# Reordering the rounds of a fused attention and routing pipeline: the division of the outputs, the turns of x and of the normed rows, and two stores

## The reference

```
xn = layernorm(x)
cq, ckv = xn @ Wc + bc, xn @ Wckv + bckv                 # 128 wide each
q = [cq @ Wcq | rope(cq @ Wqr)]                          # 16 heads x 48
k = [ckv @ Wck | rope(xn @ Wkr)];  v = ckv @ Wv          # v: 16 heads x 32
scores[i, j] = q_i . k_j / sqrt(48)                      # 16 x 16 for each token
x = x + layernorm((softmax(scores) @ v) @ Wo + bo)
xf = layernorm(x)
w = softmax(xf @ gate_w.T);  top 6 of 64 experts per token, capacity 128 each
y = sum of the chosen experts' FFN(xf) * w  +  shared FFN(xf)
out = x + layernorm(y)
```

## Time and profile before

| | |
|---|---|
| median of 3 runs | 2039.34 us (2036.21 to 2047.08) |
| profiled execution | 2034.23 us, span of the instructions 2032.2 us |
| PE, PE weight loads | busy 1816.6 us (89%), 1423.7 us (70%) |
| DVE, ACT, POOL | busy 1490.3 us (73%), 1038.9 us (51%), 557.1 us (27%) |
| mean granted clock of PE | 0.974 of full speed |

### The profile page before, as it was taken

One profiled execution on the slowest core, in us unless ns is written; L12 is line 12 of the kernel. 1 busy time (PEld: TensorE's weight loads), 2 busy tenths in 40 slices (PEclk: granted clock), 3 DMA queues, 4 the chain that ended last, 5 costly groups with the idle time before them and its releaser, 6 DMA issues. The chain is left out here.

```text
span 2032.2 us, 50014 instructions
## 1 busy us (share of the span) xinstructions
PE 1816.6 (89%) x14529; PEld 1423.7 (70%) x14529; DVE 1490.3 (73%) x3935; ACT 1038.9 (51%) x2257; POOL 557.1 (27%) x773
## 2 busy tenths in 40 slices
PE   5799999999999999999999999974899999988886
PEld 4678888888888887888888888864455555546664
DVE  6678888888888888888888888863444444429997
ACT  4555656666665656666665656651222323223333
POOL 1111212111121212111121212110344444427776
PEclk8899999999999999999999999997899999989998
DMA  5345555555555555555555555546999999979994
GB/s 188 72 122 147 132 148 133 149 128 130 144 131 150 130 147 132 145 133 134 145 127 149 128 149 132 136 133 192 338 294 288 298 288 309 292 197 395 404 394 174
DMA packets 540056, 384.01 MB, mean 189 GB/s; under 512 B 423848, under 2 KB 432168, under 8 KB 539944
## 3 DMA queue, kind: packets, MB, share of 16 engines
q1 hardware_dynamic: 519456, 324.99, 55.7%
q0 software_dynamic: 14336, 35.66, 7.5%
q10 hardware_dynamic: 6208, 22.68, 2.9%
HBM read 232.46 MB, written 150.63 MB: 189 GB/s over the span
## 5 line engine op out<-in xcount | busy, mean ns | idle before, releaser
L615 ACT COPY kT<-bank 48x256 f32<-48x256 f32 x512 | 308.7, 603 | 11.0
L890 POOL TENSOR_SCALAR ve<-mv 128x1 f32<-128x1 f32 x192 | 42.2, 220 | 893.6 <-DVE mv L725 893.6
L457 PE MATMUL bank<-wgu,xfT 128*128 128x416 f32 x512 | 193.2, 377 | 18.6 <-ACT xfT L615 18.2
L615 ACT COPY qT<-bank 48x256 f32<-48x256 f32 x512 | 187.8, 367 | 33.9 <-PE bank L450 23.0
L1097 PE MATMUL e_gu<-w,xgT 128*128 128x384 f32 x512 | 183.5, 502 | 15.4 <-DMA w<-w_ed 12.4
L458 PE MATMUL bank<-wgu,xfT 128*128 128x416 f32 x512 | 183.1, 358 | 0.0
L908 POOL TENSOR_TENSOR x<-yn,xres 128x512 f32<-128x512 f32 x64 | 81.6, 1275 | 238.5 <-DVE yn L729 238.5
L1097 PEld LDWEIGHTS e_gu<-w,xgT 128*128 128x128 f32 x512 | 92.9, 191 | 74.1 <-DMA w<-w_ed 9.9
L1258 DVE SCALAR_TENSOR_TENSOR tanh<-tanh,e_gu 128x192 f32<-128x192 f32 x64 | 22.7, 354 | 165.8 <-ACT tanh L1184 165.8
L1341 POOL DMA_INDIRECT acc_scratch<-eo,sidx x64 | 101.5, 1586 | 121.4 <-ACT eo L1180 105.9
L1120 PE MATMUL e_ps<-w,hidT 96*128 96x512 f32 x256 | 127.7, 621 | 1.6 <-ACT hidT L1172 0.9
(11 more groups left out here) (178 smaller groups left out, 4849.9 us busy)
## 6 DMA issues: line engine op xcount, KB each, us to landing
w<-w_eg SPq DMA_DIRECT2D x60, 768.0 KB
acc_scratch<-zero SPq DMA_DIRECT2D x130, 256.0 KB, 4.2
w<-w_ed SPq DMA_DIRECT2D x60, 384.0 KB
xf_scratch<-xf SPq DMA_DIRECT2D x64, 288.0 KB, 2.1
xin<-x SPq DMA_DIRECT2D x64, 256.0 KB, 3.0
v_scratch<-v SPq DMA_DIRECT2D x64, 256.0 KB, 3.7
vbd<-v_scratch SPq DMA_DIRECT2D x128, 128.0 KB, 3.3
o_scratch<-o SPq DMA_DIRECT2D x256, 64.0 KB, 2.3
```

Source lines behind the costliest of these rows:

```text
L457: nc.tensor.matmul(dst, a[:, 0], b[:, 0], start=(n == 0), stop=False)
L615: nc.scalar.copy(dst, src).then_inc(done.sem, 1)
```

## The change

The operations stay the same; their order changes, with the waits in front of them.

- PE: the turn of the normed rows moves from behind the latents to the head of the round. The turn of `xn` moves from ahead of the turn of `prob` to behind the `wck` product, ahead of PV. The rank product moves ahead of PV.
- ACT: the copy of `xfT` moves to the head of the round, the exp of the gates from ahead of the `probT` copies to behind the copy of `xT`.
- DVE: the low part of `xfT` moves up behind the first statistics. `chosen`, `ssum` and `srec` move ahead of `y`. The division follows `k` directly. The low part of `xT` falls behind the division, `erec` and the scaling of the gates to the end of the round.
- SP: the stores of `xf` and `h` move from the end of round i (tile i-5) to the next round (tile i-6), between the four stores of `o` and the wait for their landing.

```diff
--- before.py
+++ after.py
@@ -364,6 +364,14 @@
                     for g in range(2):
                         for b in range(2):
                             sp.dma_start(dst[g, b], src[64 * g:64 * g + 64, b]).then_inc(o_out.sem, 16)
+                if active(i - 6):
+                    sp.wait_ge(d_r.sem, d_r.at(i - 6))
+                    settle(sp)
+                    sp.dma_start(rows(xf_d, i - 6), xf[:, par, :]).then_inc(xf_out[par].sem, 16)
+                    sp.wait_ge(d_h.sem, d_h.at(i - 6))
+                    settle(sp)
+                    sp.dma_start(rows(h_d, i - 6), h[:, par]).then_inc(h_out[par].sem, 16)
+                if active(i - 3):
                     sp.wait_ge(o_out.sem, o_out.at(i - 3))
                     settle(sp)
                     sp.wait_ge(pe_oT.sem, pe_oT.at(i - 4))
@@ -413,13 +421,6 @@
                     src = v_d[1 - par].rearrange("(cg b t) (j d) -> b (t j) cg d", cg=NBLK, b=2, j=H)
                     for b in range(2):
                         sp.dma_start(vbd[64 * b:64 * b + 64, 1 - par, :, b, :], src[b]).then_inc(v_in[1 - par].sem, 16)
-                if active(i - 5):
-                    sp.wait_ge(d_r.sem, d_r.at(i - 5))
-                    settle(sp)
-                    sp.dma_start(rows(xf_d, i - 5), xf[:, 1 - par, :]).then_inc(xf_out[1 - par].sem, 16)
-                    sp.wait_ge(d_h.sem, d_h.at(i - 5))
-                    settle(sp)
-                    sp.dma_start(rows(h_d, i - 5), h[:, 1 - par]).then_inc(h_out[1 - par].sem, 16)
                 if isinstance(i, int) and i == NT + 2:
                     for n in range(2):
                         sp.wait_ge(rank_out[n].sem, rank_out[n].at(NT - 18 + n))
@@ -495,6 +496,10 @@
             def iteration(i, par):
                 latents = b5, [xT[:, :, n, :] for n in range(KD)], [wlat[:, :, n, :] for n in range(KD)]
                 normed = [xfT[:, :, n, :] for n in range(KD)]
+                if active(i - 5):
+                    pe.wait_ge(d_ln[2].sem, d_ln[2].at(i - 5))
+                    pe.wait_ge(a_pT.sem, a_pT.at(i - 3, 1))
+                    transposes(s0, [xf[:, 1 - par, n * P:(n + 1) * P] for n in range(KD)], pe_xfT)
                 if active(i - 2):
                     pe.wait_ge(d_q.sem, d_q.at(i - 2))
                     pe.wait_ge(d_latT.sem, d_latT.at(i - 1))
@@ -521,10 +526,6 @@
                 if active(i):
                     pe.wait_ge(d_xT.sem, d_xT.at(i))
                     low(*latents, pe_lat)
-                if active(i - 5):
-                    pe.wait_ge(d_ln[2].sem, d_ln[2].at(i - 5))
-                    pe.wait_ge(a_pT.sem, a_pT.at(i - 3, 1))
-                    transposes(s0, [xf[:, 1 - par, n * P:(n + 1) * P] for n in range(KD)], pe_xfT)
                 if active(i - 1):
                     pe.wait_ge(a_latT.sem, a_latT.at(i - 1))
                     pe.wait_ge(d_k.sem, d_k.at(i - 2))
@@ -566,10 +567,6 @@
                     pe.wait_ge(d_lat.sem, d_lat.at(i))
                     pe.wait_ge(d_oT.sem, d_oT.at(i - 3))
                     transposes(b3, [lat[:, n * P:(n + 1) * P] for n in range(2)], pe_latT)
-                if active(i + 1):
-                    pe.wait_ge(d_ln[0].sem, d_ln[0].at(i + 1))
-                    pe.wait_ge(a_kT.sem, a_kT.at(i - 2))
-                    transposes(b2, [xn[:, n * P:(n + 1) * P] for n in range(KD)], pe_xT)
                 if active(i - 2):
                     pe.wait_ge(a_exp.sem, a_exp.at(i - 2, 1))
                     pr = prob[:].rearrange("p n t h -> p (n t h)")
@@ -579,6 +576,15 @@
                 if active(i - 1):
                     pe.wait_ge(d_v.sem, d_v.at(i - 1))
                     product(b6, [latT[:, 1 - par, :, 1, :]], [wck[:, :, 0, :]], d_latT, i - 1, pe_k)
+                if active(i + 1):
+                    pe.wait_ge(d_ln[0].sem, d_ln[0].at(i + 1))
+                    pe.wait_ge(a_kT.sem, a_kT.at(i - 2))
+                    transposes(b2, [xn[:, n * P:(n + 1) * P] for n in range(KD)], pe_xT)
+                if active(i - 5):
+                    pe.wait_ge(d_r.sem, d_r.at(i - 5, 7))
+                    pe.wait_ge(a_pT.sem, a_pT.at(i - 2))
+                    nc.tensor.matmul(rank_ps, chosen[:], tri[:], start=True, stop=True).then_inc(pe_rank.sem, 1)
+
                 if active(i - 2):
                     pe.wait_ge(a_pT.sem, a_pT.at(i - 2))
                     pe.wait_ge(d_q.sem, d_q.at(i - 1, 1))
@@ -593,11 +599,6 @@
                                                     vbd[:, par, 2 * n + g].rearrange("p b d -> p (b d)"),
                                                     start=True, stop=True)
                     last.then_inc(pe_pv.sem, 1)
-                if active(i - 5):
-                    pe.wait_ge(d_r.sem, d_r.at(i - 5, 7))
-                    pe.wait_ge(a_pT.sem, a_pT.at(i - 2))
-                    nc.tensor.matmul(rank_ps, chosen[:], tri[:], start=True, stop=True).then_inc(pe_rank.sem, 1)
-
             pipeline(pe, iteration)
 
 
@@ -629,6 +630,10 @@
                     split(i)
                 if isinstance(i, int) and i == 2:
                     act.wait_ge(part_lo, len(parts))
+                if active(i - 5):
+                    act.wait_ge(pe_xfT.sem, pe_xfT.at(i - 5))
+                    act.wait_ge(pe_gu.sem, pe_gu.at(i - 6))
+                    copy(xfT[:, 0].rearrange("p k t -> p (k t)"), s0, a_xfT)
                 if active(i - 2):
                     act.wait_ge(pe_s.sem, pe_s.at(i - 3))
                     act.wait_ge(pe_qT.sem, pe_qT.at(i - 2, 1))
@@ -640,10 +645,6 @@
                     act.wait_ge(pe_kT.sem, pe_kT.at(i - 2, 1))
                     by_token = kT.rearrange("p (c t) (m a) -> p a m c t", t=B4, a=2)
                     spread(by_token, b3, a_kT, 0)
-                if active(i - 5):
-                    act.wait_ge(pe_xfT.sem, pe_xfT.at(i - 5))
-                    act.wait_ge(pe_gu.sem, pe_gu.at(i - 6))
-                    copy(xfT[:, 0].rearrange("p k t -> p (k t)"), s0, a_xfT)
                 if active(i - 2):
                     act.wait_ge(pe_kT.sem, pe_kT.at(i - 2, 2))
                     spread(by_token, b2, a_kT, 1)
@@ -668,10 +669,6 @@
                     act.wait_ge(pe_latT.sem, pe_latT.at(i))
                     act.wait_ge(pe_k.sem, pe_k.at(i - 2))
                     copy(latT[:, par, 0].rearrange("p k t -> p (k t)"), b3[:, 0:2 * P], a_latT)
-                if active(i - 5):
-                    act.wait_ge(d_r.sem, d_r.at(i - 5, 4))
-                    nc.scalar.activation(ex[:], lg[:, 0:E], ACT.Exp, bias=ntop[:, 0:1],
-                                         accum_out=esum[:, 0:1]).then_inc(a_gate.sem, 1)
                 if active(i - 2):
                     act.wait_ge(pe_pv.sem, pe_pv.at(i - 3))
                     for n, b in enumerate((s0, s1)):
@@ -681,6 +678,10 @@
                     act.wait_ge(pe_xT.sem, pe_xT.at(i + 1))
                     act.wait_ge(pe_lat.sem, pe_lat.at(i))
                     copy(xT[:, 0].rearrange("p k t -> p (k t)"), b2, a_xT)
+                if active(i - 5):
+                    act.wait_ge(d_r.sem, d_r.at(i - 5, 4))
+                    nc.scalar.activation(ex[:], lg[:, 0:E], ACT.Exp, bias=ntop[:, 0:1],
+                                         accum_out=esum[:, 0:1]).then_inc(a_gate.sem, 1)
                 if active(i - 5):
                     act.wait_ge(pe_rank.sem, pe_rank.at(i - 5))
                     act.wait_ge(rank_out[1 - par].sem, rank_out[1 - par].at(i - 7))
@@ -753,6 +754,9 @@
                 if active(i + 1):
                     dve.wait_ge(x_in[1 - par].sem, x_in[1 - par].at(i + 1))
                     stats(0, xin[:, 1 - par, :], i + 1)
+                if active(i - 5):
+                    dve.wait_ge(a_xfT.sem, a_xfT.at(i - 5))
+                    low_part(xfT, s0, d_xfT)
                 if active(i - 4):
                     dve.wait_ge(g_x1.sem, g_x1.at(i - 4))
                     stats(2, x1[:], i - 4)
@@ -775,9 +779,6 @@
                 if active(i + 1):
                     dve.wait_ge(pe_xT.sem, pe_xT.at(i))
                     normalise(0, xn[:], xin[:, 1 - par, :], i + 1)
-                if active(i - 5):
-                    dve.wait_ge(a_xfT.sem, a_xfT.at(i - 5))
-                    low_part(xfT, s0, d_xfT)
                 if active(i - 1):
                     dve.wait_ge(pe_v.sem, pe_v.at(i - 1))
                     dve.wait_ge(v_out.sem, v_out.at(i - 2))
@@ -830,6 +831,18 @@
                     dve.wait_ge(d_r.sem, d_r.at(i - 5, 5))
                     settle(dve)
                     nc.vector.match_replace(lgr[:], rep[:], lg[:], -3.0e38).then_inc(d_r.sem, 1)
+                if active(i - 5):
+                    dve.wait_ge(d_r.sem, d_r.at(i - 5, 6))
+                    dve.wait_ge(pe_rank.sem, pe_rank.at(i - 6))
+                    nc.vector.tensor_tensor(chosen[:], lgr[:, 0:E], lg[:, 0:E], ALU.not_equal).then_inc(d_r.sem, 1)
+                if active(i - 2):
```

(36 more changed lines are left out.)

## The result

The changed kernel takes 1981.5 us (median of 4 runs, 1979.2 to 1989.5) against 2042.2 us (2036.2 to 2047.1) for the kernel before in the same comparison: a ratio of 0.9711, 95% interval 0.9671 to 0.9751. On a second chip it is 1982.9 against 2052.4 us, 0.9662 (0.9632 to 0.9691). The prediction was 1984 (1962 to 2020), faster.

What follows compares the result with a forecast made beforehand. Three loops, PE with ACT (19.4 to 19.8 us), through `latT` (19.88) and through `o` (19.98), were taken to give a period of 19.95 instead of 20.86; over 58 rounds 53 us, plus 2 outside: 1984 us, range 1962 to 2020.

Steps and rivals of the forecast that it cites:

- the two waits of PE: Idle PE weight loads per round, 0.87 us before PV and 0.67 us before the turn of `oin`: what a reordering can win.
- PE's stream from scores to round start: Scores to the round's start on PE: 11.08 us before, forecast 9.74 to 10.17 without the waits before PV and `oin`.
- my bounds of 0.46 and 0.89: PE's wait before PV, taken as gone: worth 0.46 to 0.89 us a round, by matmuls or by loads.
- The round start to the scores: PE's first transposes to the scores, set by ACT running without a gap: stays 9.62 us.
- the turn of the normed rows at the head wins nothing: On PE, the short wait for `xfT` before gate/up vanishes but wins nothing, since the scores wait for ACT either way.
- the loop through `latT`: Scores, DVE's low part of `latT`, PE's turn of `q`, ACT's copies, next scores: allows a period of 19.88 us.
- PE with ACT: PE's scores to round start plus ACT's round start to scores: allows a period of 19.36 to 19.79 us.
- The loop through `o`: Scores, DVE's division `o`, stores and loads through HBM, turn of `oin`: allows 19.88 us, 19.98 with 0.1 for the stores.
- The way through HBM: End of `o` on DVE to PE's turn of `oin`, by four stores and four loads: taken as 9.2 us.
- My sign of being wrong: End of `o` to the turn of `oin`: 9.0 to 9.3 us expected; growing past 9.7 would show the forecast wrong.
- The stores' 0.1 us of traffic: Delay of `oin` by the `xf` and `h` stores ahead of its loads: 0.1 us taken, bounds nothing to 2.4.
- rivals 2 and 4: 2: stores or a missed wait delay `oin`, near 2017 us, chance 0.20; 4: store landings delay it, 2060 to 2121, 0.08.

## Why the prediction was right, and where it was not

**The period.** 19.95 was predicted, 19.93 measured; the 58 rounds times the difference, plus 2 us outside, is the gain. This was the right frame: all of it lies in the period.

**What bound before.** My sentence that the two waits of PE are what a reordering can win was wrong for one of them. The turn of `xn` alone wins nothing; the period of before was the loop `oin`, `y`, `o`, HBM, `oin`, which I used only for the kernel after. DVE's and SP's part breaks it twice: `o` comes sooner, and `y` no longer waits for `wo`; no run shows what each of the two is worth. The wait before PV costs only once that is done: 1998.9 us (20.28) with DVE's part, 1989.3 (20.09) with PE's moves before PV as well.

**PE's stream from scores to round start.** 9.74 to 10.17 predicted, 10.34 measured. The filled wait before PV is worth about 0.3 us (10.61 in the run of DVE's and SP's part, where PE waits before PV and not for `oin`), below both of my bounds of 0.46 and 0.89: the rank product and PV each keep 0.17 to 0.19 us of idle loads in front of them. The term was mis-sized.

**The round start to the scores.** 9.62 predicted, 9.52 measured, with ACT without a gap: right. That the turn of the normed rows at the head wins nothing is nearly right; what it does is to stand where PE else waits for `latT`.

**DVE.** The low part of `latT` ends 10.30 us after the scores (10.50 predicted), `o` starts at 10.86 (11.01), both 0.15 to 0.2 too late in my sum. The way from DVE to PE is 0.11 us, not 0.25 (run with the turn where it was). So the loop through `latT`, which I made one of the longest at 19.88, does not bind, and the wait that I forecast for it is not there. That this error and the one before PV have opposite signs is why the sum is so close. The agreement to 0.02 us is luck to that extent: my 19.95 came from two loops of 19.88 and 19.98, of which one does not bind and the other only in some rounds. PE with ACT, which I put at 19.79 at most, holds most rounds at 10.34 + 9.52 = 19.86. What the reasoning earned is the direction and the size to about 0.1 us a round.

**The loop through `o`.** 19.88 plus 0.1 predicted. It does bind, but only in some rounds: one of ten in the first profile (5 of 52), a third on the second chip. The way through HBM was right: from the end of `o` to the last landing it is 9.13 us on the first chip and 9.37 on the second, where I had 9.2 and 0.1 for the stores. With the 0.04 us from landing to turn the loop would allow 10.86 + 0.68 + 9.13 + 0.04 - 1.12 = 19.59 us on the first chip and 19.83 on the second, close below PE with ACT. My sign of being wrong was badly chosen. From the end of `o` to the turn of `oin` it is 9.6 us (9.7 on the second chip), not 9.0 to 9.3, but in most rounds `oin` has landed by then and PE comes later, so this distance does not measure the way.

The stores' 0.1 us of traffic is right within what these runs tell, and rivals 2 and 4 are rejected at this place: the landing of `oin` is 2.5 to 2.7 us with one set of stores, with one more, and with none. What a further store costs is its issue on SP, 0.41 us. Their place on SP matters much more: the total is 181 us over the kernel before with them at the end of the queue, 12 us over it with them behind the loads.

**The ends.** 1 us or less for the late store is not seen apart from the scatter of the last part.

## What to carry to other kernels

Add up the loops that cross engines and HBM before the waits of one engine: a wait on the busiest engine is worth its time only if filling it shortens the longest loop, and one run with that edit alone shows it. When DMAs are moved in a queue, price first what they wait for and who waits for their buffer, and only then their bytes; a queue's own wait for a landing is a free place for issues that are ready, as long as they fit in it (two fit in 1.44 us here; a third made the loads 0.41 us later). When the longest loop is shortened, others lie close behind (here 19.86 and 19.6 to 19.8 us), so the next edit moves the wait rather than the time unless it shortens them together.

## What the runs showed of the hardware that was not expected

The kernel before differs between chips by 10 to 12 us (medians 2042, 2052, 2054 and 2052), the changed one by 1 us on two of them (1981.5, 1982.9). From the start of `o` to the turn of `oin` it is 9.5 to 10.7 us within one run of the kernel before, and its period follows that way directly. The same changed kernel has 9.13 us from the end of `o` to the last landing on the first chip and 9.37 on the second, which fits; that this makes the difference between chips for the kernel before is argued, not shown, since its trace is from one chip alone.

From the end of the low part of `latT` on DVE to PE's next load it is 0.11 us; from ACT's last `kT` to the scores 0.12 us in the round shown, where it was 0.32 before (medians 0.16 and 0.29).

PE's granted clock has a mean of 0.92 from 600 to 1000 us in the run with the stores at the end (0.86 to 1.00 in stretches of 25 us, so it is at the lower level, 1.2 GHz, for part of the time), where PE waits 2.7 us a round for `oin`. In all the other runs it is 0.99 or 1.00 there.
